# A linear attention beside a stack of local attentions: the first chunk's V copies go out early, and half of its Q is made ahead of the last output

## The chip, the cores and the metric

One core of one Trainium2 chip. The metric is the device time of one launch in microseconds, on the profiled core; the kernel is one program, with all data in SBUF between its start and its end except for the weights, the rotary tables and one copy of the input that is kept in DRAM.

## The reference

Input is x, 2048 tokens of 128 features. With xn the layer norm of x, the output is x + A(xn) + B(xn).

```python
def A(xn):                      # 8 heads of 16, one sequence of 2048
    q, k, v, gate = (xn @ W.T for W in (Wq, Wk, Wv, Wg))
    q, k = rope(q), rope(k)
    kv, ksum, vsum = einsum('bshd,bshe->bhde', k, v), k.sum(1), v.sum(1)
    o = (q @ kv * scale + vsum) / (q @ ksum * scale + 2048)
    return ((o + depthwise_conv5(v)) * gate) @ Wo.T

def B(x):                       # 6 layers, 16 heads of 64, windows of 32 tokens
    for i in range(6):
        q, k, v = split(shift_tokens(x) @ Wqkv[i], 3)
        q, k = l2norm(q) * qs, l2norm(k) * ks
        q, k = rope_xpos(q), rope_xpos(k)
        # each window of 32 queries sees its own 32 keys and the 32 before
        x = softmax(q @ k.T * 8 + mask) @ v @ Wo[i] + x
        x = ffn(shift_tokens(x)) + x       # layer norm, gated GELU, 341 wide
    return x
```

All is float32; some products are made of three matmuls on a high and a low part of each operand.

## The kernel before

**The start.** The input comes in as 16 tiles of 128 tokens. It is normalised on DVE and transposed into XA (128 features x 2048 tokens). Then A is computed: first Q, K and V of all tokens with the sums over K and V, then, in four groups (g = 0 to 3) of 512 tokens, the output. For a group TensorE makes the denominator and the numerator (`m_sums`), the convolution of V (`m_conv`, five matmuls, two records each in the trace), the gate (`m_gate`) and the output projection (`m_out`). ACT adds 2048 to the denominator (`m_den`). DVE inverts it and multiplies (`m_ratio`), adds the convolution and multiplies by the gate (`m_mix`, into `o1`), and adds the projection to the input (`m_add`, counted in `x1_done`). The sum x1 is written to DRAM (`scratch`) by one DMA and fetched again at the end.

**Chunks.** B runs over 6 layers x 8 chunks of 256 tokens, numbered m = 0 to 47. The work of a chunk is cut into steps: `a_...` is projection and preparation of Q, K and V, `b_...` scores, softmax and attention, `c_...` output projection and feed-forward part. A table, `SCHEDULE`, gives one order of steps, which every engine walks through with those of its own: in iteration `it` an a-step belongs to chunk `it`, a b-step to `it` - 1 and a c-step to `it` - 2, and `+1` behind a name means one chunk ahead. Each engine has its own instruction stream, and semaphores (named `..._done`, `..._in`) are all that ties them. `EARLY` names the steps of chunk 0 that aren't issued from the table because they are written out by hand between the group steps of A, as `a_v(0, 0)` and the like.

**Steps of a chunk that matter here.** `a_v`(m, c): V of half c on TensorE (6 matmuls of 512 columns, three for each half of the heads). `a_vs`: ACT copies it from PSUM to Vs, for which chunk m must wait until the V copies of chunk m - 1 have landed (`v2_in`). `windows`(m): SP issues 16 copies from Vs to V2, which lay V out by windows; V2 has two buffers, m % 2. `halo`(m): two more, the last window into the other buffer. `a_x`, `a_y`(m, p): a quarter of K (p = 0, 1) or Q (p = 2, 3) into PSUM bank 0 and 1; `a_mx`, `a_my`: DVE multiplies it by the rotary tables into UV; `a_sqx`, `a_sqy`: ACT squares it; `a_rot`: POOL adds up the rotated halves, into Kt or Qt (the first half of Qtb). `a_norm`, `a_rck`, `a_lnk`, `a_rh`, `a_rl`, `a_sp`: the K norms' inverse roots, spread over the partitions through TensorE; `a_kn`: DVE scales Kt by them. `keys`(m) and `queries`(m): SP issues 8 copies each, Kt to Kb and Qt to Qb. `b_s`(m, i): mask and scores on TensorE, which wait for `k_in` and `q_in`. `a_xs`, `a_xh`, `a_xl`: the shifted input of the next chunk and its high and low part, on ACT, ACT and POOL.

**SP's queue** is one stream, in program order; an instruction that waits holds all behind it. Before the chunks it ends in `keys(0)`, the write of x1 to `scratch` once `x1_done` is 4, and a wait until that has landed:

```python
keys(0)
e.wait_ge(s["x1_done"], G1)
e.dma_start(a["scratch"]..., xt).then_inc(s["scratch_out"], 16)
e.wait_ge(s["scratch_out"], 16)
for m in range(N):
    ...
    windows(m)
    if m:
        keys(m)
    queries(m)
    halo(m)
```

**Memory.** The start borrows space. `xt` (the input, later x1), `xn`, the convolution's weights `wc` and `lrow` lie in V2, whose first buffer is columns 0 to 4095 of `V2flat` and whose second is 4096 to 8191 (S is 2048). Input and normalised input fill the first buffer, so `windows(0)` can't be issued until the write of x1 has read it. `qT`, A's transposed Q, lies in the half of Qtb where chunk 0's Qt goes; `a_rot(0, 2)` waits for `x1_done`.

Of the kernel before, what the change touches and what calls it, by code (L numbers as in the profile page):

```python
# [18 lines left out]
S = 2048  # L19
D = 128  # L20
# [3 lines left out]
NCH = S // P  # L24
T1 = 512
G1 = S // T1
# [15 lines left out]
KLEPE = 5  # L42
# [23 lines left out]
    a_x1 a_y1 a_mx1 a_my1 a_sqy1 a_sqx1 a_rot1 a_norm0 a_sum0 a_rck0 a_lnk0 a_rh0 a_rl0 a_sp0 a_sp1 a_kn0 a_kn1""".split()  # L66
# [64 lines left out]
def program(nc, a):  # L131

    with ExitStack() as ctx:
# [60 lines left out]
        V2flat = V2[:, :, :, :].rearrange("p a w n -> p (a w n)")  # L194
        xt = V2flat[:, 0:S].rearrange("p (c n) -> p c n", c=NCH)
        xn = V2flat[:, S:2 * S].rearrange("p (c n) -> p c n", c=NCH)
        wc = V2flat[:, 2 * S:2 * S + KLEPE * D].rearrange("p (i n) -> p i n", i=KLEPE)
        lrow = V2flat[:, 2 * S + KLEPE * D:2 * S + 2 * KLEPE * D].rearrange("p (i n) -> p i n", i=KLEPE)
# [38 lines left out]
        def _(e):  # L237
# [98 lines left out]
            tables(1)  # L336
            keys(0)
            e.wait_ge(s["x1_done"], G1)
            e.dma_start(a["scratch"].rearrange("(c p) n -> p c n", p=P), xt).then_inc(s["scratch_out"], 16)
            e.wait_ge(s["scratch_out"], 16)  # L340
            for m in range(N):
                l, g = m // G, m % G
                if 0 < m < N - 1:
                    tables(m + 1)
                if g == 1 and l:
                    weights_b(l)
                if g == 2 and l:
                    weights_d(l)
                windows(m)
                if m:  # L350
                    keys(m)
                queries(m)
                halo(m)
                if g == 0 and l + 1 < DEPTH:
                    weights_a(l + 1)
                if g == 2 and l + 1 < DEPTH:
                    weights_c(l + 1)
# [10 lines left out]
        def _(e):  # L368
# [297 lines left out]
            a_v(0, 0)  # L666
            m_conv(0)
            m_sums(0)
# [21 lines left out]
            m_gate(3)  # L690
            m_out(3)
# [6 lines left out]
        def _(e):  # L698
# [221 lines left out]
            m_mix(3)  # L920
            m_add(3)
# [6 lines left out]
        def _(e):  # L928
# [193 lines left out]
            a_rh(0, 0)  # L1122
            run({"w_h": w_h, "c_wh": c_wh, "a_xs": a_xs, "a_xh": a_xh, "a_halo": a_halo, "a_vs": a_vs, "a_sqy": a_sqy, "a_sqx": a_sqx,
# [4 lines left out]
        def _(e):  # L1128
# [41 lines left out]
            def a_rot(m, p):  # L1170
# [3 lines left out]
                if m == 0 and p == 2:  # L1174
                    e.wait_ge(s["x1_done"], G1)
# [32 lines left out]
            a_rl(0, 0)  # L1208
            run({"b_nrm": b_nrm, "w_l": w_l, "c_wl": c_wl, "c_zl": c_zl, "a_xl": a_xl, "a_halo": a_halo, "a_rot": a_rot, "a_rl": a_rl, "b_sub": b_sub},
# [45 lines left out]
```

## Time and profile before

| what | value |
|---|---|
| median of 3 runs | 1840.32 us (1836.89 to 1849.28) |
| profiled execution, its own time | 1832.69 us |
| its span in the trace | 1831.1 us |
| mean granted clock of TensorE | 0.969 |
| instructions | 80253 |

The trace is of the profiled execution, and its times count from the start of the span. Engines are PE (TensorE matmuls), PEld (its weight loads), DVE, ACT, POOL; SPq is SP's queue issuing DMAs. Names in a row are tiles, output first: ps is PSUM, V stands for V2 and Vs's copies as well as for the input that lies in V2, E for the scores and, at the start, for A's intermediate results, Qtb at the start also for A's weights. Nearly all matmuls have the line of the helper `mm` (L370) and nearly all activations that of `act` (L930), so they are told apart by tile and shape. Behind a row of the timeline stands the idle time of the engine before it, and what ended it.

### The profile page before, as it was taken

Reading aid. Unit: us, or ns where it says so; the run is one execution under the profiler, and the core shown is the slowest. Engines: PE = TensorE matmul, PEld = TensorE weight load, DVE = VectorE, ACT = ScalarE, POOL = GpSimd, SP = SyncE. Lnnn points to the kernel's source line nnn. Section 1 sums busy time; section 2 is a strip of 40 time slices with the busy share of each in tenths; the row PEclk is TensorE's granted clock in tenths of the full one; section 3 lists DMA queues with packets and bytes.
Section 4 is the critical chain, followed back from the end, with each engine's and each line's share of the span. In section 5 each row is a group of like instructions: output and inputs, shape, how many; then the busy total and the mean of one; then the engine's idle time right before and its main releaser. Section 6 shows DMA issues by size and latency. Waiting matters only on the chain.

```text
span 1831.1 us, 80253 instructions
## 1 busy us (share of the span) xinstructions
PE 1654.4 (90%) x35762; PEld 1360.0 (74%) x35762; DVE 1217.9 (67%) x1910; ACT 1139.4 (62%) x2115; POOL 1000.9 (55%) x757
## 2 busy tenths in 40 slices
PE   5858999989989998899999999999999989999986
PEld 4447778777777877778777787777778777778775
DVE  7656677666657766666766775676677676677562
ACT  2225676657656766666766666576566676667653
POOL 2135466656545656655674664585566475566441
PEclk9979999999999999999999999999999999999996
DMA  3085665665655567556557655557655665665650
GB/s 124 12 199 126 165 145 132 149 170 127 152 136 134 127 157 194 114 130 158 133 125 194 154 129 138 139 130 188 162 129 128 152 141 123 154 152 127 140 120 24
DMA packets 98585, 253.25 MB, mean 138 GB/s; under 512 B 30016, under 2 KB 36288, under 8 KB 97472
## 3 DMA queue, kind: packets, MB, share of 16 engines
q1 hardware_dynamic: 98240, 248.12, 56.8%
q8 instruction: 281, 4.60, 1.1%
q14 instruction: 64, 0.52, 0.1%
HBM read 44.59 MB, written 2.10 MB: 25 GB/s over the span
## 4 chain that ended last, share of the span: by engine, by line
PE 54%; DVE 11%; issue 9%; ACT 9%; SPq 8%; DMA 2%; POOL 0%; ACTq 0%; DVEq 0%; POOLq 0%
PE ps L370 49%; DVE E L841 4%; SPq L317 4%; PE ps L539 4%; SPq L328 4%; DVE rs L851 3%; DVE UV L780 2%; ACT E L930 2%; ACT zs L930 2%; DMA Qtb<-Qtb 2%; ACT PT L930 1%; ACT sq L930 1%; ACT Vs L930 1%; PE ps L492 1%; ACT R L930 1%
## 5 line engine op out<-in xcount | busy, mean ns | idle before, releaser
L780 DVE SCALAR_TENSOR_TENSOR UV<-ps,veca,rope 128x512 f32<-128x512 f32 x768 | 526.7, 743 | 192.4 <-PE ps L370 191.5
L1183 POOL TENSOR_TENSOR Kt<-UV 128x512 f32<-128x512 f32 x192 | 240.8, 1275 | 446.5 <-DVE UV L780 445.3
L930 ACT ACTIVATE sq<-ps 128x512 f32<-128x512 f32 (+1 forms) x400 | 231.5, 579 | 321.7 <-PE ps L370 303.4
L1183 POOL TENSOR_TENSOR Qtb<-UV 128x512 f32<-128x512 f32 x192 | 242.6, 1286 | 123.5 <-DVE UV L780 123.5
L1193 POOL TENSOR_TENSOR E<-E,mx 128x1024 f32<-128x1024 f32 x96 | 182.7, 1903 | 148.4 <-DVE mx L847 148.4
L370 PE MATMUL ps<-xh,wh 128*128 128x256 f32 x768 | 242.2, 315 | 6.0 <-issue 4.4
L370 PE MATMUL ps<-xh,wl 128*128 128x256 f32 x768 | 221.9, 289 | 1.8 <-issue 1.8
L370 PE MATMUL ps<-xl,wh 128*128 128x256 f32 x768 | 221.5, 288 | 1.9 <-issue 1.9
L370 PEld LDWEIGHTS ps<-PT,V 64*64 64x64 f32 x12288 | 198.7, 135 | 31.6 <-issue 19.3
L370 PE MATMUL ps<-Kb,Qtb 64*32 64x64 f32 (+1 forms) x12288 | 189.3, 223 | 34.6 <-issue 34.5
L370 PE MATMUL ps<-PT,V 64*64 64x32 f32 x12288 | 215.9, 221 | 1.5 <-ACT PT L930 0.7
L370 PEld LDWEIGHTS ps<-Kb,Qtb 64*32 64x32 f32 x12288 | 154.0, 106 | 63.2 <-issue 63.0
L370 PE MATMUL ps<-OT,wo 128*128 128x128 f32 x1536 | 194.8, 281 | 4.4 <-issue 4.4
L1202 POOL TENSOR_TENSOR E<-E,ri 128x1024 f32<-128x1024 f32 x96 | 182.8, 1905 | 21.8 <-DVE ri L853 21.6
L370 PEld LDWEIGHTS ps<-OT,wo 128*128 128x128 f32 x1536 | 187.5, 199 | 5.1 <-issue 4.9
L370 PEld LDWEIGHTS ps<-xh,wh 128*128 128x128 f32 x768 | 150.9, 196 | 49.6 <-issue 26.5
L930 ACT ACTIVATE Vs<-ps 128x512 f32<-128x512 f32 x192 | 114.6, 598 | 92.1 <-PE ps L370 73.3
L851 DVE TENSOR_REDUCE rs<-E 128x16 f32<-128x1024 f32 x96 | 117.1, 1220 | 62.3 <-ACT E L930 62.3
L841 DVE TENSOR_TENSOR E<-ps,rq 128x1024 f32<-128x1024 f32 x96 | 114.9, 1197 | 64.6 <-PE ps L370 64.2
L539 PE MATMUL ps<-ident,E 128*128 128x128 f32 x768 | 123.0, 283 | 37.5 <-ACT PT L930 35.2
L370 PEld LDWEIGHTS ps<-xl,wh 128*128 128x128 f32 x768 | 151.7, 198 | 4.0 <-issue 4.0
L370 PEld LDWEIGHTS ps<-xh,wl 128*128 128x128 f32 x768 | 151.9, 198 | 2.8 <-issue 2.7
(129 smaller groups left out, 3324.1 us busy)
## 6 DMA issues: line engine op xcount, KB each, us to landing
V<-Vs SPq DMA_DIRECT2D x672, 128.0 KB
Kb<-Kt SPq DMA_DIRECT2D x384, 128.0 KB
Qtb<-Qtb SPq DMA_DIRECT2D x384, 128.0 KB, 2.4
rope<-in_c_rope SPq DMA_DIRECT2D x48, 512.0 KB
raw<-in_Wqkv SPq DMA_DIRECT2D x6, 1536.0 KB, 6.9
V<-Vs SPq DMA_DIRECT2D x96, 64.0 KB
V<-V SPq DMA_DIRECT2D x96, 64.0 KB, 2.0
wo<-in_Wo SPq DMA_DIRECT2D x6, 512.0 KB, 5.9
```

The lines of the kernel that those rows point to most:

```text
L317: e.dma_start(Kb[p0:p0 + W, j0:j0 + HQ, :], Kt[hq * W:(hq + 1) * W, half, :, :]).then_inc(s["k_in"], 16)
L328: e.dma_start(Qb[p0:p0 + W, j0:j0 + HQ, :], Qt[hq * W:(hq + 1) * W, half, :, :]).then_inc(s["q_in"], 16)
L370: return e.matmul(out, lhsT, rhs, start=start, stop=stop, **kw)
L492: ins = e.transpose(ps[:, NORM, T + c * P:T + (c + 1) * P], R[:, 1, c * P:(c + 1) * P], ident[:, :])
L539: ins = e.transpose(ps[:, PTB, h * P:(h + 1) * P], E[:, c, i % 2 * HQ + h, :, :], ident[:, :])
L780: e.scalar_tensor_tensor(UV[:, p % 2, slot, :].rearrange("p (i t) -> p i t", i=2), ps[:, half, :].rearrange("p (i t) -> p i t", i=2), veca ...
L841: e.tensor_tensor(E[:, c].rearrange("p j r k -> p r j k"), ps[:, 2:4, :].rearrange("p r (j k) -> p r j k", k=KEYS), by_row.unsqueeze(3).br ...
L851: e.tensor_reduce(rs[:, c], heads(E[:, c]), AX.X, ALU.add).then_inc(s["rs_done"], 1)
L930: return e.activation(out, in_, f, **kw)
L1183: e.tensor_tensor(dst, u, v, op).then_inc(s["rot_done"], 1)
L1193: e.tensor_tensor(ev, ev, mx[:, c].unsqueeze(2).broadcast_to([P, H, KEYS]), ALU.subtract).then_inc(s["sub_done"], 1)
L1202: e.tensor_tensor(ev, ev, ri[:, c].unsqueeze(2).broadcast_to([P, H, KEYS]), ALU.mult).then_inc(s["pn_done"], 1)
```

## The change

SP issues `windows(0)` right behind the tables, ahead of `keys(0)`, and no longer waits for the write of x1 ahead of the chunks; that wait stands ahead of `windows(1)`. To free the first buffer of V2, the input (`xt`) moves to the last quarter of V2, `wc` and `lrow` to behind the first 512 columns of the second buffer (which `halo(0)` writes), and `xn`, which is read early, to the front. The steps of the third quarter of chunk 0 (`a_x2` to `a_rot2`, half of its Q) join `EARLY`, and are written out ahead of `m_out(3)` on TensorE, `m_add(3)` on DVE and in the corresponding places on ACT and POOL. `a_rot(0, 2)` waits for the last numerator (`nm_done`), which is the last to read `qT`, instead of x1. On TensorE `m_sums(0)` goes ahead of `m_conv(0)`.

```diff
--- before.py
+++ after.py
@@ -63,7 +63,8 @@
     c_wl w_h2 c_fin c_down w_l2 b_oto1""".split()
 LAG = {"w": 0, "a": 0, "b": 1, "c": 2}
 EARLY = """a_xs0 a_xh0 a_xl0 a_halo0 a_v0 a_vs0 a_v1 a_vs1 a_x0 a_y0 a_mx0 a_my0 a_sqy0 a_sqx0 a_rot0
-    a_x1 a_y1 a_mx1 a_my1 a_sqy1 a_sqx1 a_rot1 a_norm0 a_sum0 a_rck0 a_lnk0 a_rh0 a_rl0 a_sp0 a_sp1 a_kn0 a_kn1""".split()
+    a_x1 a_y1 a_mx1 a_my1 a_sqy1 a_sqx1 a_rot1 a_norm0 a_sum0 a_rck0 a_lnk0 a_rh0 a_rl0 a_sp0 a_sp1 a_kn0 a_kn1
+    a_x2 a_y2 a_mx2 a_my2 a_sqy2 a_sqx2 a_rot2""".split()
 
 
 def part(token):
@@ -192,10 +193,11 @@
         hf = D // 2
 
         V2flat = V2[:, :, :, :].rearrange("p a w n -> p (a w n)")
-        xt = V2flat[:, 0:S].rearrange("p (c n) -> p c n", c=NCH)
-        xn = V2flat[:, S:2 * S].rearrange("p (c n) -> p c n", c=NCH)
-        wc = V2flat[:, 2 * S:2 * S + KLEPE * D].rearrange("p (i n) -> p i n", i=KLEPE)
-        lrow = V2flat[:, 2 * S + KLEPE * D:2 * S + 2 * KLEPE * D].rearrange("p (i n) -> p i n", i=KLEPE)
+        xt = V2flat[:, 3 * S:4 * S].rearrange("p (c n) -> p c n", c=NCH)
+        xn = V2flat[:, 0:S].rearrange("p (c n) -> p c n", c=NCH)
+        w0 = 2 * S + 512
+        wc = V2flat[:, w0:w0 + KLEPE * D].rearrange("p (i n) -> p i n", i=KLEPE)
+        lrow = V2flat[:, w0 + KLEPE * D:w0 + 2 * KLEPE * D].rearrange("p (i n) -> p i n", i=KLEPE)
         xr = raw[:, 0:S].rearrange("p (c n) -> p c n", c=NCH)
         Qt = Qtb[:, 0, :, :, :]
         Qb = Qtb[:, 1, :, :, :].rearrange("p h j t -> p (h j) t")
@@ -334,10 +336,10 @@
             weights_d(0)
             tables(0)
             tables(1)
+            windows(0)
             keys(0)
             e.wait_ge(s["x1_done"], G1)
             e.dma_start(a["scratch"].rearrange("(c p) n -> p c n", p=P), xt).then_inc(s["scratch_out"], 16)
-            e.wait_ge(s["scratch_out"], 16)
             for m in range(N):
                 l, g = m // G, m % G
                 if 0 < m < N - 1:
@@ -346,8 +348,10 @@
                     weights_b(l)
                 if g == 2 and l:
                     weights_d(l)
-                windows(m)
+                if m == 1:
+                    e.wait_ge(s["scratch_out"], 16)
                 if m:
+                    windows(m)
                     keys(m)
                 queries(m)
                 halo(m)
@@ -664,8 +668,8 @@
                 ins.then_inc(s["y1_done"], 1)
 
             a_v(0, 0)
+            m_sums(0)
             m_conv(0)
-            m_sums(0)
             a_v(0, 1)
             m_gate(0)
             m_sums(1)
@@ -688,6 +692,8 @@
             a_sp(0, 0)
             a_sp(0, 1)
             m_gate(3)
+            a_x(0, 2)
+            a_y(0, 2)
             m_out(3)
 
             run({"a_v": a_v, "a_x": a_x, "a_y": a_y, "a_norm": a_norm, "a_sp": a_sp, "b_rqt": b_rqt, "b_s": b_s, "b_pt": b_pt,
@@ -918,6 +924,8 @@
             a_kn(0, 0)
             a_kn(0, 1)
             m_mix(3)
+            a_mx(0, 2)
+            a_my(0, 2)
             m_add(3)
 
             run({"a_mx": a_mx, "a_my": a_my, "a_rck": a_rck, "b_rcq": b_rcq, "a_kn": a_kn, "b_rq": b_rq, "b_scale": b_scale,
@@ -1120,6 +1128,8 @@
             m_den(3)
             a_lnk(0, 0)
             a_rh(0, 0)
+            a_sqy(0, 2)
+            a_sqx(0, 2)
             run({"w_h": w_h, "c_wh": c_wh, "a_xs": a_xs, "a_xh": a_xh, "a_halo": a_halo, "a_vs": a_vs, "a_sqy": a_sqy, "a_sqx": a_sqx,
                  "a_lnk": a_lnk, "b_lnq": b_lnq, "a_rh": a_rh, "b_exp": b_exp, "b_pto": b_pto, "b_oto": b_oto, "c_xs": c_xs,
                  "c_zsq": c_zsq, "c_rs": c_rs, "c_zh": c_zh, "c_gelu": c_gelu}, lambda g: None)
@@ -1172,7 +1182,7 @@
                 if p == 0:
                     e.wait_ge(s["sel_done"], 4)
                 if m == 0 and p == 2:
-                    e.wait_ge(s["x1_done"], G1)
+                    e.wait_ge(s["nm_done"], G1)
                 if m and p % 2 == 0:
                     e.wait_ge(s["k_in" if p == 0 else "q_in"], m * 128)
                 q = 2 * (p % 2)
@@ -1206,6 +1216,7 @@
             a_rot(0, 0)
             a_rot(0, 1)
             a_rl(0, 0)
+            a_rot(0, 2)
             run({"b_nrm": b_nrm, "w_l": w_l, "c_wl": c_wl, "c_zl": c_zl, "a_xl": a_xl, "a_halo": a_halo, "a_rot": a_rot, "a_rl": a_rl, "b_sub": b_sub},
                 lambda g: None)
 
```

How it stands in each stream. SP, from the rotary tables of the start to the first chunk's Q copies (Vs to V: V copies; Kt to Kb: K copies; Qtb to Qtb: Q copies), before:

```order
L281 DMA rope<-in_c_rope 128x1024 x2
L317 DMA Kb<-Kt 32x1024 x8
L339 DMA scratch<-V 128x16x128
L292 DMA V<-Vs 32x1024 x4
L295 DMA V<-Vs 32x1024 x3
L297 DMA V<-Vs 32x512
L292 DMA V<-Vs 32x1024 x4
L295 DMA V<-Vs 32x1024 x3
L297 DMA V<-Vs 32x512
L328 DMA Qtb<-Qtb 32x1024 x8
L305 DMA V<-V 32x512 x2
```

and now:

```order
L283 DMA rope<-in_c_rope 128x1024 x2
L294 DMA V<-Vs 32x1024 x4
L297 DMA V<-Vs 32x1024 x3
L299 DMA V<-Vs 32x512
L294 DMA V<-Vs 32x1024 x4
L297 DMA V<-Vs 32x1024 x3
L299 DMA V<-Vs 32x512
L319 DMA Kb<-Kt 32x1024 x8
L342 DMA scratch<-V 128x16x128
L330 DMA Qtb<-Qtb 32x1024 x8
L307 DMA V<-V 32x512 x2
```

The V copies stand ahead of the K copies, and between the write and the Q copies nothing is left.

DVE, from the last denominator to the norms of chunk 0's Q (L780, now L786, are the multiplications by the rotary tables, four for each quarter; the row with V is the addition that makes x1), before:

```order
L809 TENSOR_SCALAR R<-ps 128x256
L772 TENSOR_TENSOR V<-ps,V 128x512
L824 TENSOR_TENSOR Kt<-ps,Kt 128x2x512 x2
L762 SCALAR_TENSOR_TENSOR E<-ps,Qtb,E 128x512
L767 TENSOR_TENSOR E<-ps,E 128x512
L772 TENSOR_TENSOR V<-ps,V 128x512
L780 SCALAR_TENSOR_TENSOR UV<-ps,veca,rope 128x512 x8
L809 TENSOR_SCALAR R<-ps 128x256
```

and now:

```order
L815 TENSOR_SCALAR R<-ps 128x256
L778 TENSOR_TENSOR V<-ps,V 128x512
L830 TENSOR_TENSOR Kt<-ps,Kt 128x2x512 x2
L768 SCALAR_TENSOR_TENSOR E<-ps,Qtb,E 128x512
L773 TENSOR_TENSOR E<-ps,E 128x512
L786 SCALAR_TENSOR_TENSOR UV<-ps,veca,rope 128x512 x4
L778 TENSOR_TENSOR V<-ps,V 128x512
L786 SCALAR_TENSOR_TENSOR UV<-ps,veca,rope 128x512 x4
L815 TENSOR_SCALAR R<-ps 128x256
```

Four of the eight multiplications stand ahead of the last addition.

TensorE, between the first and the second half of chunk 0's V (the rows with XA,V are the convolution, those with Qtb alone denominator and numerator), before:

```order
L370 MATMUL ps<-wl,xh 128x512
L370 MATMUL ps<-XA,V 128x512
L370 MATMUL ps<-XA,V 128x510
L370 MATMUL ps<-XA,V 128x511
L370 MATMUL ps<-XA,V 128x512 x2
L370 MATMUL ps<-Qtb 128x512 x2
L370 MATMUL ps<-wh,xh 128x512
```

and now:

```order
L374 MATMUL ps<-wl,xh 128x512
L374 MATMUL ps<-Qtb 128x512 x2
L374 MATMUL ps<-XA,V 128x512
L374 MATMUL ps<-XA,V 128x510
L374 MATMUL ps<-XA,V 128x511
L374 MATMUL ps<-XA,V 128x512 x2
L374 MATMUL ps<-wh,xh 128x512
```

The two matmuls of the sums went ahead of the five of the convolution.

## Rows read from the trace of the kernel before

**Rows 1.** The page, busy time by engine.

```profile
PE 1654.4 (90%) x35762; PEld 1360.0 (74%) x35762; DVE 1217.9 (67%) x1910; ACT 1139.4 (62%) x2115; POOL 1000.9 (55%) x757
```

**Rows 2.** The table by stretch: busy us and instructions, granted clock, DMA share, GB/s.

```profile
60.00:80.00 20.00, 18.94 (x75) 11.00 (x75) 19.36 (x19) 4.96 (x8) 2.50 (x2) 1.00 0.01 2
...
110.00:120.00 10.00, 3.27 (x9) 2.66 (x10) 0.00 (x0) 1.98 (x4) 0.00 (x0) 0.50 0.86 192
...
171.00:207.00 36.00, 33.78 (x805) 28.22 (x807) 26.46 (x41) 25.25 (x49) 22.07 (x17) 1.00 0.65 152
```

**Rows 3.** The chain in order of time: start, us, what.

```profile
97.98 5.40 DMA scratch<-V
...
114.04 2.02 DMA V<-Vs
```

**Rows 4.** Timeline of TensorE: start, us, engine, line, operation, tiles, shape.

```profile
60.51 1.02 PE L370 MATMUL ps<-XA,Qtb 128*128 128x512 f32 x2
...
63.45 1.13 PE L370 MATMUL ps<-Qtb 128*128 128x512 f32 x2 [1.06 <-DVE E L757]
...
89.74 0.36 PE L370 MATMUL ps<-Rh,sel 128*128 128x256 f32 x1 [0.40 <-issue]
...
94.34 1.86 PE L370 MATMUL ps<-Qtb,E 128*128 128x128 f32 x8 [2.55 <-DVE E L767]
...
106.32 0.80 PE L370 MATMUL ps<-wh,xh 128*128 128x512 f32 x1 [2.39 <-POOL xl L1161]
...
108.62 0.63 PE L370 MATMUL ps<-wl,xh 128*128 128x512 f32 x1
116.73 0.80 PE L370 MATMUL ps<-wh,xh 128*128 128x512 f32 x1 [7.48 <-ACT Vs L930]
...
122.08 0.41 PE L370 MATMUL ps<-mask,identb 32*32 32x512 bf16 x8
122.41 0.21 PE L370 MATMUL ps<-Kh,Qtb 64*32 64x32 f32 x1
```

**Rows 5.** Timeline of ACT.

```profile
60.02 1.29 ACT L930 ACTIVATE Vs<-ps 128x512 f32<-128x512 f32 x2 [0.87 <-PE ps L370]
```

**Rows 6.** Timeline of SP's queue; a row's us hold the issues and waits between.

```profile
13.02 32.41 SPq L281 DMA_DIRECT2D rope<-in_c_rope  x2
...
92.87 5.06 SPq L317 DMA_DIRECT2D Kb<-Kt  x8
...
114.68 5.04 SPq L328 DMA_DIRECT2D Qtb<-Qtb  x8
```

**Rows 7.** Timeline of DVE.

```profile
90.49 2.36 DVE L824 TENSOR_TENSOR Kt<-ps,Kt 128x1024 f32<-128x1024 f32 x2 [2.49 <-PE ps L370]
...
96.24 0.69 DVE L772 TENSOR_TENSOR V<-ps,V 128x512 f32<-128x512 f32 x1 [1.95 <-PE ps L370]
97.59 1.41 DVE L780 SCALAR_TENSOR_TENSOR UV<-ps,veca,rope 128x512 f32<-128x512 f32 x2 [0.66 <-PE ps L370]
...
100.77 2.90 DVE L780 SCALAR_TENSOR_TENSOR UV<-ps,veca,rope 128x512 f32<-128x512 f32 x4 [0.20 <-PE ps L370]
```

**Rows 8.** Timeline of POOL.

```profile
103.09 2.49 POOL L1183 TENSOR_TENSOR Qtb<-UV 128x512 f32<-128x512 f32 x2 [0.54 <-DVE UV L780]
105.54 0.72 POOL L1161 TENSOR_TENSOR xl<-xs,xh 128x256 fp32r<-128x256 f32 x1
```

**Rows 9.** The page, DMA issues: count, KB each, us to landing.

```profile
Qtb<-Qtb SPq DMA_DIRECT2D x384, 128.0 KB, 2.4
```

**Rows 10.** TensorE's waits, the chain, queues in 127 to 131, a stretch.

```profile
PE ps L370 <- issue: 52.8, 38, 3.3
...
127.35 3.28 issue
...
q8 instruction: 1, 0.02, 1.8%
...
131.00:136.00 5.00, 5.00 (x97) 3.90 (x83) 4.64 (x7) 1.80 (x5) 3.76 (x3) 0.66 1.04 211
```

## The prediction

> **What bounds the kernel now.** I read the page first. TensorE is busy 90% of the span [rows 1], so time goes where it stands idle or where it is the last to finish. The table by stretch then shows that the start is unlike the rest [rows 2]: in 110 to 120 us TensorE is busy for 3.27 of 10 us at a granted clock of 0.50 (all of it at the lower level, 1.2 GHz), DVE and POOL do nothing, and the DMA rings are busy for 0.86. From 171 us on TensorE is busy 33.78 of 36 us. The change touches only what is done once, in the first 125 us, so its worth is read there.
>
> The chain of waits goes through this place without a gap [rows 3]: SP issues the write of x1 to DRAM at 97.98, waits 5.40 us for it to land, then issues the first chunk's 16 V copies, and the last lands 2.02 us after 114.04, at 116.06. That releases ACT (V of chunk 1 out of PSUM into Vs, which the copies read), and that releases TensorE at 116.73, after 7.48 us of idleness [rows 4]. From there the chain is TensorE work, then chunk 1's K, Q and attention: each chunk follows from the one before, and no row shows a resource with a clock of its own. What comes off here should come off the end.
>
> **SP: V copies ahead of K copies, no wait for the write.** The V of chunk 0 is complete in Vs when ACT's pair from 60.02, 1.29 us long, ends at 61.31 [rows 5]. SP was through with its start-up loads at 45.43 (13.02 + 32.41, nearly all of it a wait) and then stood until the K copies at 92.87 [rows 6]. The 16 V copies take 16 x 0.63 = 10.1 us of issue (8 Q copies take 5.04 [rows 6]) and 2.0 to land: 61.4 to about 73.6, in a stretch where the rings' share is 0.01 [rows 2]. They cost nothing while they end before the K copies, at 92.87 less what the rest gains; more than 17 us of cover are left. What makes room for them, the input, the convolution's weights and the normalised input in other columns of V2, adds and moves no instruction. K copies are issued for 5.06 us as before, then the write, then SP goes straight to the Q copies. The wait for the write (5.40) stands now ahead of chunk 1's V copies, which come later anyway; the write lands before them. So the release at 116.06 goes and the 7.48 us go, if nothing else is late. Term C: 7.5, with 7.48 as the row gives it; below it only by what stands under "what is late next".
>
> **Half of Q ahead of the last output.** DVE finishes the key scaling (pair from 90.49) at 92.85, does the last mix, then idles 1.95 us for TensorE's last output, 0.66 for the first Q projection and 0.20 for the third [rows 7]: 2.8 us. Now its four Q multiplications stand between mix and output. Their projections need only PSUM banks 0 and 1, which the two key scalings free (about 1.2 and 2.36 us after their start), and TensorE has nothing else: it waits for the mix 2.55 us before 94.34 [rows 4]. Each projection is six matmuls of 256 columns. The six of 512 columns from 106.32 to 108.62 are 0.46 apart at the low clock [rows 4]; half the columns make 0.23, and six 1.4 us, an estimate. So the first is ready before DVE ends the mix, and TensorE is through with both soon after it and turns to the output. DVE runs through: four multiplications (2.9 as a row of four), the addition (0.69), four more. ACT's squares of the same PSUM banks fit beside them. The second pair of projections could be late by up to 0.7 us at the low clock. Term B: 2.8, bounds 2.0 (0.7 off for that, rounded) and 2.9. The output's addition ends about 0.8 us earlier than before in spite of the four, so the write is not held up: it follows the K copies, as before. POOL makes this half of Q before the other half, beside DVE, at the same length per pair; its new condition, the last numerator instead of x1, is met before. ACT makes xs of chunk 1 later, at about 95; what needs it, POOL's xl at 105.54, stands behind the last Q rotation anyway [rows 8].
>
> **Sums before convolution.** TensorE's first convolution stood ahead of the first sums, for which DVE waits. With the order turned DVE's first reciprocal begins earlier, but the first output still needs the gate, which TensorE issues at 60.51 behind the second V projection [rows 4], and that has not moved. What is gained is the idle 1.06 us before 63.45 and the turn it started: TensorE reaches its second numerator at about 61.8 instead of 63.45. It then has work without a gap of note (18.94 of the 20 us from 60 to 80 [rows 2]) up to R's broadcast at 89.74, where its own idle time is 0.40. So that broadcast and the key scaling come 1.6 us earlier. Term A: 1.6; 0 if DVE or ACT hold the chain at its old time, and no more than 1.6, as TensorE has no idle time to give.
>
> **What is late next.** With A + B = 4.4 the last Q rotation (POOL, pair from 103.09, end 105.58 [rows 8]) ends at 101.2 and xl at 101.9, so TensorE starts V of chunk 1 at 101.9 instead of 106.32 and goes on into its second half after 2.8 us (six times 0.46), in place of 116.73. Its work up to the scores of chunk 0 (122.08 masks, 122.41 first score) is then 11.9 us earlier, at 110.5. The scores also need Q: issued from 101.2, 5.04 us of issue, 2.4 to land [rows 6, 9], 108.6. So Q has 1.9 us to spare and is the next bound: whatever else gets faster here, the gain ends at 13.8. Chunk 1's V copies, behind Q copies and the next layer's weights, come about as much earlier as the scores do; their readers are a chunk later.
>
> **Sum:** 1.6 + 2.8 + 7.5 = 11.9 us. The profiled execution took 1832.69 (span 1831.1), so it would take 1820.8. That execution is 7.6 below the median of the three runs shown, 1840.32; taken off that median, the forecast is 1828.4. Own bounds: 0 + 2.0 + 7.5 = 9.5 and 13.8, so 1826.5 to 1830.8 on the same scale.
>
> **A rule against it.** TensorE stood 3.28 us at 127.35 "for nothing the profile shows"; the one packet of the instruction queue in 127 to 131 us is 0.02 MB [rows 10]. I read this as program code that came late. Moved copies could then uncover such a load elsewhere: in 61 to 73 us TensorE has few instructions (75 matmuls in 60 to 80 [rows 2]), so one at most, 3.3 off the gain.
> The Trainium skill, "Runtime: NRT & Kernel Launch", section Instruction fetch mechanics, says the opposite of such loads: the sequencer fetches the next block while it executes, and crossing a block is "mostly hidden". By that page the early copies cost nothing at all and the sum stays 11.9; by the row it could be 8.6. The same row shows the page's rule not holding at 127.35, if the packet is its cause.
>
> **Rivals.**
> 1. The write of x1 takes the place of the V copies. Now the Q copies follow it without a wait; it is issued at about 97 and lands 5.4 later, at 102.4, just as the Q copies start. If they are held by the whole 5.4, less the 1.9 they have to spare, 3.5 are lost: gain 8.4, 1831.9. For it: the rings share. Against: they overlap for 1.4 us only. 0.13.
> 2. More goes than the idle time. TensorE, no longer idle from 109 to 116.7, keeps the high clock up to the scores (gain 13.8, where Q caps it), the 3.28 us vanish, and the matmuls of 131 to 136, granted 0.66 [rows 10], gain 5 x 0.34 = 1.7: 18.8, 1821.5. Against: TensorE still waits from about 96 to 101.9 for most of the time, as before 106.32. 0.12.
> 3. The gain is used up inside chunk 1: some chain that hangs on the early part alone, not on the scores, sets its end; then A + B alone or less arrive, 0 to 4.4: 1836 to 1840. Against: the chain runs through the scores of chunk 0. 0.08. That the copies don't leave early would end here too; the order of SP says they do.
> 4. Slower: late code loads. The trace has 38 idle times of TensorE without a releaser, 52.8 us, the longest 3.3 [rows 10]. If SP's copies, now about 1.5 us ahead of TensorE's work in the early chunks, meet more of them, each costs the mean, 52.8 / 38 = 1.4. Nine use up the gain (11.9 / 1.4), 22 make it slower by 1%, and with 30 of the 48 chunks hit it is 30 x 1.4 - 11.9 = 30 slower, 1870. Against: each chunk's V copies wait for its own V, which sets the distance anew. 0.04.
> Forecast: 0.63.
>
> **Chances.** 1% (18.4 us) is about what a measurement of this kernel can tell from no change. Rival 2 is faster by more, and the three runs shown differ by 12.4, so a gain of 12 can be read as more than 18: faster 0.17. Forecast, rivals 1 and 3: same 0.80. Slower 0.03. The range: 1818 takes in rival 2 and some noise of the median, 1839 rivals 1 and 3 nearly whole.
>
> **What would show it.** After: no idle time of TensorE over 3 us between 103 and 120; V copies issued from 61.4; Q copies from 101; DVE without idle time from the key scaling to the last of eight multiplications; first score at 110.5; chunk spacing and busy shares unchanged after that. A wait for Q copies longer than 1 us before the scores speaks for rival 1, a first score before 109 for rival 2, unchanged end times with early scores for rival 3, a sum of releaserless idle time well above 52.8 for rival 4. Wrong altogether if the time differs by less than 4 or more than 20 us.

## The result, and the profile after

Over 14 runs of each on the same chips, the changed kernel took 1824.95 us in the median (1813.93 to 1842.36) and the kernel before 1838.81 (1827.73 to 1851.03). The ratio is 0.9912, 95% interval 0.9885 to 0.994: faster by 16 us, between 11 and 21. One of the 14, the longest, ran in a slower state and isn't in the ratio. A second measurement further down gave 0.9928 (0.99 to 0.9957), 13 us. The forecast was 11.9 off the time before, 1828.4 us; the time lies in its range, and the gain at the low end of the interval. My own bounds on the gain were 9.5 to 13.8; the medians differ by 13.9, and the two ratios give 13 and 16, so the gain is near the upper bound or above it. The profiled execution took 1818.27 us (span 1816.5), where that of before took 1832.69 (1831.1).

SP's queue after, from the V copies of chunk 0 on (start, us from first issue to last, line, tiles, count):

```profile
62.79 2.52 SPq L294 DMA_DIRECT2D V<-Vs  x4
...
73.60 0.60 SPq L299 DMA_DIRECT2D V<-Vs  x1
92.99 4.96 SPq L319 DMA_DIRECT2D Kb<-Kt  x8
98.00 0.59 SPq L342 DMA_DIRECT2D scratch<-V  x1
102.22 5.67 SPq L330 DMA_DIRECT2D Qtb<-Qtb  x8
```

The V copies end 19 us before the K copies start, as forecast. Against [rows 6], the Q copies start 12.5 us earlier, as POOL's last rotation ends (102.19, below), and no wait for the write stands before them. But their issue takes 5.67 us instead of 5.04.

TensorE after, the rows that answer to [rows 4]:

```profile
50.57 0.77 PE L374 MATMUL ps<-wh,xh 128*128 128x512 f32 x1 [3.60 <-POOL xl L1171]
...
89.86 0.35 PE L374 MATMUL ps<-Rh,sel 128*128 128x256 f32 x1 [0.40 <-issue]
...
94.46 1.16 PE L374 MATMUL ps<-Qtb,E 128*128 128x128 f32 x8 [0.46 <-DVE E L773]
96.40 0.38 PE L374 MATMUL ps<-xh,wh 128*128 128x256 f32 x1 [0.79 <-ACT sq L938]
...
102.93 0.50 PE L374 MATMUL ps<-wh,xh 128*128 128x512 f32 x1 [2.22 <-POOL xl L1171]
...
105.03 0.63 PE L374 MATMUL ps<-wh,xh 128*128 128x512 f32 x1
...
109.13 0.41 PE L374 MATMUL ps<-mask,identb 32*32 32x512 bf16 x8
109.70 0.21 PE L374 MATMUL ps<-Kh,Qtb 64*32 64x32 f32 x1 [0.16 <-DMA Qtb<-Qtb]
```

The 7.48 us of idleness before V's second half are gone: it starts at 105.03, right behind the first, where before it started at 116.73. The first score comes at 109.70 instead of 122.41. And its row names a new wait, 0.16 us for the Q copies: these are now the last to arrive, if only just. The two projections for Q's first half (ahead of 94.46) fill most of the time in which TensorE waited 2.55 us for the mix; 0.46 are left.

DVE and POOL after, for [rows 7, 8]:

```profile
90.61 2.35 DVE L830 TENSOR_TENSOR Kt<-ps,Kt 128x1024 f32<-128x1024 f32 x2 [2.50 <-PE ps L374]
...
94.32 2.72 DVE L786 SCALAR_TENSOR_TENSOR UV<-ps,veca,rope 128x512 f32<-128x512 f32 x4
96.95 0.68 DVE L778 TENSOR_TENSOR V<-ps,V 128x512 f32<-128x512 f32 x1
97.55 2.72 DVE L786 SCALAR_TENSOR_TENSOR UV<-ps,veca,rope 128x512 f32<-128x512 f32 x4
```

```profile
99.69 2.50 POOL L1193 TENSOR_TENSOR Qtb<-UV 128x512 f32<-128x512 f32 x2 [0.64 <-DVE UV L786]
102.15 0.72 POOL L1171 TENSOR_TENSOR xl<-xs,xh 128x256 fp32r<-128x256 f32 x1
```

Behind the scaling of the keys, none of DVE's rows has an idle time before it up to the eighth multiplication. But the scaling itself starts at 90.61, no earlier than the 90.49 of [rows 7], although the sums went ahead; why, the experiment with the convolution first shows.

The page, busy time by engine, and the table by stretch (as [rows 1, 2]):

```profile
PE 1650.2 (91%) x35762; PEld 1358.0 (75%) x35762; DVE 1220.4 (67%) x1910; ACT 1140.8 (63%) x2115; POOL 1001.9 (55%) x757
```

```profile
60.00:80.00 20.00, 20.00 (x80) 11.90 (x79) 16.39 (x18) 4.96 (x8) 2.50 (x2) 1.00 0.44 100
100.00:110.00 10.00, 7.62 (x83) 5.39 (x72) 2.23 (x5) 3.97 (x8) 2.87 (x3) 0.83 0.83 203
110.00:120.00 10.00, 7.64 (x316) 5.38 (x296) 8.66 (x12) 3.58 (x7) 7.59 (x6) 0.87 0.94 275
...
171.00:207.00 36.00, 34.06 (x801) 28.00 (x800) 24.60 (x38) 24.63 (x46) 20.93 (x17) 1.00 0.67 154
```

The V copies have filled an empty stretch (the share of time in which the DMA rings are busy is 0.44 instead of 0.01 in 60 to 80) beside a TensorE that is never idle there. The counts of instructions are as before and the later chunks nearly so; the granted clock of 110 to 120 us is 0.87 instead of 0.50. Finer stretches show when TensorE's clock fell and came back. Before:

```profile
104.00:105.00 1.00, 0.00 (x0) 0.00 (x0) 0.42 (x1) 0.00 (x0) 1.00 (x2) 0.92 0.51 115
...
121.00:122.00 1.00, 1.00 (x6) 0.93 (x5) 0.92 (x2) 0.14 (x1) 0.00 (x0) 0.54 0.50 129
```

and after:

```profile
103.00:104.00 1.00, 1.00 (x4) 0.84 (x5) 0.00 (x0) 0.00 (x0) 0.00 (x0) 0.84 0.67 147
...
107.00:108.00 1.00, 1.00 (x8) 0.87 (x7) 0.00 (x0) 0.58 (x2) 0.00 (x0) 0.95 0.83 184
```

Before, it fell to the lower level (1.2 GHz) at about 104.8 us, ahead of the first half of chunk 1's V, and stayed there through that half, the idle time and the second half, until about 121.9. After, it fell at about 103.7, in that first half, and was back at about 107.1.

The chain of after at the same place:

```profile
97.55 2.07 DVE UV L786 x3
...
99.69 2.51 POOL Qtb L1193 x2
102.22 0.51 SPq L330
...
107.30 2.35 DMA Qtb<-Qtb
...
109.70 1.03 PE ps L374 x36
```

It no longer goes through the write and the V copies [rows 3]; it goes through DVE, POOL and the Q copies.

### The profile page after: what moved, and what is told of

It reads as the page before. It is cut to its first block, busy times and chain, and to the rows that moved or that the text cites. A ratio compares the mean times of both kernels' runs of the same rounds, so it can differ in the third digit from the quotient of the medians.

```text
span 1816.5 us, 80252 instructions
## 1 busy us (share of the span) xinstructions
PE 1650.2 (91%) x35762; PEld 1358.0 (75%) x35762; DVE 1220.4 (67%) x1910; ACT 1140.8 (63%) x2115; POOL 1001.9 (55%) x757
## 4 chain that ended last, share of the span: by engine, by line
PE 50%; DVE 12%; SPq 11%; issue 9%; ACT 9%; DMA 3%; POOL 1%; ACTq 0%; DVEq 0%; POOLq 0%
PE ps L374 46%; SPq L330 5%; SPq L319 5%; DVE E L847 4%; PE ps L543 3%; DMA Qtb<-Qtb 3%; DVE UV L786 3%; DVE rs L857 2%; ACT E L938 2%; ACT zs L938 2%; ACT PT L938 1%; DVE Kt L830 1%; ACT sq L938 1%; PE ps L496 1%; ACT Vs L938 1%
## 5 line engine op out<-in xcount | busy, mean ns | idle before, releaser
L786 DVE SCALAR_TENSOR_TENSOR UV<-ps,veca,rope 128x512 f32<-128x512 f32 x768 | 526.8, 744 | 181.1 <-PE ps L374 180.3
```

Source lines behind the costliest of these rows:

```text
L786: e.scalar_tensor_tensor(UV[:, p % 2, slot, :].rearrange("p (i t) -> p i t", i=2), ps[:, half, :].rearrange("p (i t) -> p i t", i=2), veca ...
```

## The experiments

The profiles are read by three distances, since the start of V's projection of chunk 0 (S, the first matmul of wh and xh) itself drifts between 48.99 and 52.35 us: from S to the scaling of the keys (K, DVE), from K to POOL's xl, and from K to the first score. "Stop" is TensorE's idle time without a releaser in the second half of chunk 0's scores; "chunks 0 to 4" is the time between their rows of rq.

| kernel | S | S to K | K to xl | K to first score | stop | chunks 0 to 4 | ratio to before (95%) |
|---|---|---|---|---|---|---|---|
| before | 49.88 | 40.61 | 15.05 | 31.92 | 3.28 | 136.9 | 1 |
| before again | 50.20 | 40.28 | 15.09 | 31.62 | 2.81 | 138.8 | - |
| changed | 50.57 | 40.04 | 11.54 | 19.09 | 1.87 | 138.3 | 0.9912 (0.9885-0.994) |
| changed again | 49.20 | 40.15 | 11.53 | 19.13 | 2.32 | 140.0 | 0.9928 (0.99-0.9957) |
| V late | 52.35 | 39.68 | 11.53 | 30.81 | 1.74 | 141.0 | 0.9972 (0.9934-1.0009) |
| V early alone | 48.99 | 41.79 | 15.27 | 22.55 | 1.78 | 140.1 | 0.9925 (0.9894-0.9955) |
| convolution first | 49.64 | 41.55 | 11.54 | 19.16 | 1.98 | 142.2 | 0.9886 (0.9835-0.9938) |
| Q late | 51.24 | 40.23 | 13.59 | 21.79 | 4.47 | 142.6 | 0.9911 (0.9881-0.9941) |
| V behind K | 50.93 | 39.94 | 11.54 | 28.58 | 2.48 | 141.7 | 0.9977 (0.9948-1.0006) |
| wait kept | 50.75 | 39.95 | 11.54 | 20.09 | 2.18 | 143.0 | 0.9954 (0.9912-0.9995) |
| write behind Q | 50.12 | 39.91 | 11.54 | 18.85 | 2.05 | 143.2 | 0.9945 (0.9912-0.9979) |
| weights later | 50.85 | 39.05 | 11.53 | 19.14 | 0.46 | 143.8 | 0.9971 (0.994-1.0002) |
| before, weights later | 49.48 | 40.30 | 15.10 | 31.50 | none | 142.8 | 1.0061 (1.0029-1.0094) |

The distances behind K are good to some tenths (kernels that have the same steps there agree that well); S to K moves by more, as the experiment with the convolution shows. The ratios are good to 0.3 to 0.5%, 5 to 10 us.

### V late: everything but the V copies

```diff
-            windows(0)
             keys(0)
             e.wait_ge(s["x1_done"], G1)
             e.dma_start(a["scratch"]..., xt).then_inc(s["scratch_out"], 16)
+            e.wait_ge(s["scratch_out"], 16)
+            windows(0)
```

> The changed kernel with chunk 0's V copies put back behind the write of x1 and its wait; half of Q early and the sums first are kept. Additive theory (each term is worth its size alone: 1.6 + 2.8): first score of chunk 0 near 118, 4.4 us better than before. Chain theory (the V release hangs on the K copies and the write, which those two terms do not move in this trace: K copies from 92.99, write from 98.00): V copies from about 103.4, last landing 116.1, first score 122 +- 0.7, gain 0 to 0.7 us, ratio to before 1.000.

TensorE of this kernel:

```profile
104.34 0.50 PE L375 MATMUL ps<-wh,xh 128*128 128x512 f32 x1 [2.21 <-POOL xl L1172]
...
117.56 0.80 PE L375 MATMUL ps<-wh,xh 128*128 128x512 f32 x1 [10.65 <-ACT Vs L939]
```

V's first half comes as early against K as in the changed kernel, and then TensorE idles 10.65 us instead of 7.48 for the same late release. From K to the first score it takes 30.81 us: 1.0 less than before, where B by its own size would have 3.5 less; 0.4 of that 1.0 lies behind the wait, from V's second half to the masks (4.94 us instead of 5.35). From S it is 70.5 us, against 72.5, 71.9 and 71.8 in the three profiles that have all of the start as before: 1.3 to 2.0 earlier. That is over the 0 to 0.7 of the chain theory and far under the 4.4 of the additive one. The ratio can't be told from 1. The chain theory holds for Q: making half of it early is worth little as long as the V copies are late. It does not hold for the sums: the K copies wait for the scaling of the keys, so they move with it (issued 42.1 us behind S, before 42.7 to 43.0), and the write and the V copies behind them.

### V early alone

```diff
-    a_x2 a_y2 a_mx2 a_my2 a_sqy2 a_sqx2 a_rot2"""
...
-            m_sums(0)
             m_conv(0)
+            m_sums(0)
```

with the steps of chunk 0's third quarter taken out of the hand-written part on four engines; the memory layout stays the changed one.

> Only the V copies early, in the new memory layout; Q's first half and the convolution as before. Both theories: the 7.48 us before V's second half are gone, TensorE starts V of chunk 1 at 106.3 as before, first score near 114.6 (113.0 at the earliest, where Q copies from 105.6 end), gain 7.5 to 9 us, ratio about 0.9955.

```profile
106.82 0.79 PE L373 MATMUL ps<-wh,xh 128*128 128x512 f32 x1 [1.62 <-POOL xl L1164]
...
109.55 0.50 PE L373 MATMUL ps<-wh,xh 128*128 128x512 f32 x1
...
112.99 0.41 PE L373 MATMUL ps<-mask,identb 32*32 32x512 bf16 x8
```

This one edit takes 9.2 us from K to the first score (31.8, the mean of two profiles of before, to 22.55), of 7.5 to 9 expected. 7.3 is the idle time (7.48 and 7.16 in the two), and 1.9 is clock: from the start of V's second half to the masks it takes 3.44 us, before 5.35 (116.73 to 122.08 [rows 4]). It also has most of the gain in the total.

### Convolution first

```diff
-            m_sums(0)
             m_conv(0)
+            m_sums(0)
```

> The changed kernel with the first convolution ahead of the first sums again. If the sums first are worth my 1.6: key scaling at 92.1 instead of 90.61, first score 111.3 instead of 109.7. Rival: the swap gave nothing, as the same matmuls took 6.9 us instead of 6.1 (1.5 us of start-up drift aside): key scaling within 0.5 of 90.6, first score within 0.7 of 109.7. No difference in total that a run can tell.

From S to K, the five kernels with the convolution first take 41.55, 41.79, 40.61, 40.28 and 40.30, mean 40.9; the eight with the sums first 39.05 to 40.23, mean 39.9. But this mean of 1.0 mixes two things, and cutting the distance at the second half of chunk 0's V separates them. TensorE of the kernel before, convolution, sums and the start of that half:

```profile
52.57 4.99 PE L370 MATMUL ps<-XA,V 128*128 128x512 f32 x10
57.40 1.88 PE L370 MATMUL ps<-Qtb 128*128 128x512 f32 x4
58.71 0.80 PE L370 MATMUL ps<-wh,xh 128*128 128x512 f32 x1
```

and of this one:

```profile
52.34 5.93 PE L374 MATMUL ps<-XA,V 128*128 128x512 f32 x10
58.10 1.88 PE L374 MATMUL ps<-Qtb 128*128 128x512 f32 x4
59.42 0.80 PE L374 MATMUL ps<-wh,xh 128*128 128x512 f32 x1
```

The order is the same and nothing waits, but convolution and sums take 6.14 us in one and 7.08 in the other: TensorE's clock, at its lower level behind S, came back sooner in the kernel before (granted clock of 54 to 56 us: 1.00 there, 0.67 here). Over all profiles this stretch took 5.81 to 7.32 us with the convolution first and 5.92 to 7.08 with the sums first. From the second half of chunk 0's V to K, on the other hand, the five kernels with the convolution first took 31.77 or 31.78 us and the eight with the sums first 30.41 to 30.45. So the swap is worth 1.35 us, near the 1.6, and the return of the clock, up to 1.5 us sooner or later, is laid over it. In the changed kernel's first profile it can't be seen, since its S is 0.7 late and its stretch takes 6.91. The key scaling came at 91.19 rather than the 92.1 expected, with an S 0.9 earlier than the changed kernel's; in the distance, 1.5 longer, the first theory is right. Behind K nothing changes (19.16), and in the total a microsecond can't be seen: the 0.9886 is the lowest ratio of all, and its interval, from 6 runs, holds the changed kernel's.

### Q late

```diff
-    a_x2 a_y2 a_mx2 a_my2 a_sqy2 a_sqx2 a_rot2"""
+    """
```

and, again, the same steps taken out of the hand-written part.

> The changed kernel with all of Q behind the last output again. By the sum: DVE idles about 2.8 us again, last Q rotation at about 105, first score at 112.5 to 113.8 instead of 109.7 (the high clock before the scores gone too would make it 114), gain 9 us left, ratio 0.995. Rival (Q early is hidden under the V copies' gain): first score below 111.

The first score is at 113.26, within the 112.5 to 113.8 expected, and 21.79 behind K: Q early is worth 2.7 us there. With the convolution first it is worth 3.4 (V early alone 22.55, convolution first 19.16). The prediction's 2.8 was right for one and low for the other. Again the clock is a part of it. From K to xl it takes 13.59 us here and 15.05 before, with the same steps of Q. The table by stretch for 96 to 98 us, before and here:

```profile
96.00:98.00 2.00, 2.00 (x11) 2.00 (x11) 1.10 (x2) 0.00 (x0) 0.00 (x0) 0.50 0.92 205
```

```profile
96.00:98.00 2.00, 1.90 (x17) 1.69 (x15) 1.40 (x3) 0.07 (x1) 0.00 (x0) 1.00 0.97 215
```

Here Q's projections run at the higher level, before at the lower, and DVE idles 1.8 us in place of 3.0. So against Q late, with the clock high in both, Q early takes 2.05 us out of K to xl; the other 1.5 of the 3.5 against before is what this kernel has too, and the clock is the only difference there that the trace shows. Why it was low there in the four profiles with Q late and the convolution first, and high in this one, no run separates. In the total, 0.9911 against 0.9912, three microseconds are below what these runs tell.

### Before again

> The kernel before itself, a second profile. It tells what two executions of one program differ by. Expected: the start of V's projection of chunk 0 within 1.5 us of 49.88, first score 72.5 +- 0.7 us behind it as in the profile before; from there chunk times wander against the first profile by up to 5 us either way, without a trend. If the wandering of the gain after the first chunks (11.0 to 15.3 us) belonged to the change, the two profiles of before would keep within 1 us of each other.

S is 0.3 later, the first score 71.9 behind it instead of 72.5. But the span is 1840.9, 9.8 us longer than that of the first profile of the same program, and the distance grows: 1.6 us at chunk 4, 3.3 at chunk 8, 6.3 at chunk 11, 9.9 at chunk 47. That is twice the 5 us expected, and it has a trend, which I had not expected. So a span says little of a change of 12 us, and the wandering of the changed kernel's lead against before (13.0 us at chunk 0, 11.5 at chunk 4, 9.7 at chunk 18, 15.3 at chunk 23, 10.3 at chunk 47, 14.6 at the end) is of the size by which two executions of one program differ too. Only distances inside the first 125 us, and ratios of many runs, bear on the change.

### V behind K, and the write of x1

Three kernels move SP's steps. V behind K:

```diff
-            windows(0)
             keys(0)
+            windows(0)
```

> The changed kernel with chunk 0's V copies behind the K copies, still ahead of the write and without its wait: V copies from 98.0, last landed about 110; then write, then Q copies from 108.8, landed near 117. First score near 117, 26 us behind the key scaling instead of 19.1, gain about 5.5 us, ratio 0.997. If only the wait for the write mattered and not SP's idle time before 93 us, the first score would stay near 110.

Wait kept, ahead of the Q copies:

```diff
             e.dma_start(a["scratch"]..., xt).then_inc(s["scratch_out"], 16)
+            e.wait_ge(s["scratch_out"], 16)
             for m in range(N):
```

> The changed kernel with the wait for the write of x1 put back, now ahead of the Q copies. Write issued near 98.0, landed near 103.4: the Q copies start about 1.2 us later than 102.2, but no longer share the rings with it, so their issue takes 5.0 instead of 5.67: first score 0.3 to 0.9 us later in distance from the key scaling (19.1 us now). If the order and not the wait is what counts, the total keeps all but 1 us of the gain; if the wait is the half of it, 5 us are lost.

Write behind the Q copies and the halo of chunk 0:

```diff
-            e.wait_ge(s["x1_done"], G1)
-            e.dma_start(a["scratch"]..., xt).then_inc(s["scratch_out"], 16)
...
                 halo(m)
+                if m == 0:
+                    e.wait_ge(s["x1_done"], G1)
+                    e.dma_start(a["scratch"]..., xt).then_inc(s["scratch_out"], 16)
```

> The changed kernel with the write of x1 issued behind the Q copies and the halo. Rival 1 says the write holds the Q copies: their issue falls from 5.67 to about 5.0 us, the first score comes 0.2 to 0.7 us earlier (then TensorE's own work, masks at 109.1, is last). Chunk 1's V copies wait longer for the write, to about 118 instead of 110.9, and are through by the K copies at 131; no loss. Total within 1 us of the changed kernel.

V behind K, SP and TensorE:

```profile
109.16 0.58 SPq L342 DMA_DIRECT2D scratch<-V  x1
109.79 7.43 SPq L330 DMA_DIRECT2D Qtb<-Qtb  x8
```

```profile
111.22 0.79 PE L374 MATMUL ps<-wh,xh 128*128 128x512 f32 x1 [5.67 <-ACT Vs L938]
119.45 0.21 PE L374 MATMUL ps<-Kh,Qtb 64*32 64x32 f32 x1 [3.29 <-DMA Qtb<-Qtb]
```

The position counts and not the wait alone: without SP's idle time before 93 us the V copies hold TensorE 5.67 us, then the Q copies 3.29. It was slower than expected (28.58 from K, expected 26), because the write of x1, now right ahead of the Q copies, stretches their issue to 7.43 us. That is my first rival at work. In the changed kernel they are 4.2 us behind the write and it costs 0.7 of issue: 5.67 against 4.96 in the two kernels that keep the write away (and 4.95 where the Q copies come 6 to 8 us behind it, in Q late and V early alone):

```profile
104.00 4.96 SPq L330 DMA_DIRECT2D Qtb<-Qtb  x8
```

(wait kept) and

```profile
101.64 4.96 SPq L330 DMA_DIRECT2D Qtb<-Qtb  x8
```

(write behind Q). The first starts the copies 1.8 us later and loses 1.0, a little more than the 0.3 to 0.9 expected; the second wins 0.24 and is then held by TensorE's own work (its first score comes without a wait). Neither can be told from the changed kernel in total with these intervals; both ratios are higher in their centre. Taking the write out of the Q copies' way brings nothing that could be told, and no version here can be shown to beat the changed kernel.

### Changed again, and the weights later

The stop of TensorE in chunk 0's scores [rows 10] stands in all eleven profiles of the other kernels, 1.74 to 4.47 us long. To see whether it hangs on what is in the rings, the load of the next layer's QKV weights (1.5 MB, ahead of chunk 1's V copies) was put off by one chunk, in the changed kernel and in that of before:

```diff
-                if g == 0 and l + 1 < DEPTH:
+                if g == 1 and l + 1 < DEPTH:
                     weights_a(l + 1)
```

> The changed kernel itself again, unchanged. Key scaling 39.9 to 40.2 us behind the start of V's projection, first score 18.9 to 19.2 behind the key scaling; chunk 0 to chunk 4 (row of rq to row of rq) between 138 and 143 us, TensorE idle without a releaser at the stop in the second half of chunk 0's scores between 1.9 and 4.5 us. Ratio to before between 0.9885 and 0.994, as in the first measurement.

> The changed kernel with the load of the next layer's QKV weights (1.5 MB) one chunk later in each layer, so that it no longer goes out just ahead of chunk 1's V copies. Late-code theory (the stop of TensorE in the second half of chunk 0's scores, 1.9 to 4.5 us in eight profiles, is a block of program code that arrives late behind full rings): the stop falls below 1.5 us, chunk 0 to 1 takes 34 us or less, total 2 to 4 us better than the changed kernel's second run beside it. Rival (the stop has nothing to do with what is in the rings): the stop stays at 1.9 to 4.5, total unchanged.

> The kernel before with the same later weight load. Late-code theory: the stop of 3.28 us at 127.35 falls below 1.5 us and the kernel is 2 to 4 us faster than before, ratio 0.998 to 0.999; rival: stop unchanged, ratio 1.000. Either way it stays 9 us or more behind the changed kernel, since the V release at 116 us is as late as it was.

TensorE with the weights later, in the changed kernel: at the old place (chunk 0's scores) first, and one chunk on:

```profile
114.43 1.08 PE L374 MATMUL ps<-Kb,Qtb 64*32 64x64 f32 x86 [0.46 <-issue]
...
148.58 0.58 PE L374 MATMUL ps<-xh,wh 128*128 128x256 f32 x1 [4.10 <-issue]
157.06 0.60 PE L374 MATMUL ps<-Kb,Qtb 64*32 64x64 f32 x36 [0.92 <-issue]
```

and SP's load there:

```profile
141.11 0.45 SPq L256 DMA_DIRECT2D raw<-in_Wqkv  x1
```

In the kernel before:

```profile
160.54 0.58 PE L370 MATMUL ps<-xh,wh 128*128 128x256 f32 x1 [3.51 <-issue]
```

The changed kernel's second run came out as expected in all its numbers (table). Where the weights left, the stop fell to 0.46 or went altogether (chunk 0 to 1 took 32.4 us instead of 34.3 in the changed kernel; 32.5 in that of before, instead of 33.6 and 32.9 in its two profiles). Where they went, a stop that was there already grew: at the place of the 4.10 and 3.51 us the eleven other profiles have 1.84 to 2.78. Chunk 1 to 2 took 42.0 instead of 36.4 and 41.0 instead of 35.9. The load costs more in its new place, and the totals are worse: by 0.4% against the second run of the changed kernel beside it (0.9971 and 0.9928, intervals that just overlap), and by 0.6% against before. Half of the expectation failed: the stop does hang on the traffic, but no time was won by moving it.

## Why the prediction was right, and where it was off

**The bound and the chain: right.** The release of V's second half was the piece on the path; it went, and the first score came 12.7 us earlier in the first profiles (13.4 from S), of 11.9 forecast. The V copies are hidden in SP's idle time, and V behind K shows what they cost without it.

**Term C, 7.5: too small by the clock.** TensorE took 10.41 us from V's first half to its second (106.32 to 116.73), and 2.10 after: 8.3 gone. I had the six matmuls at the low clock's 0.46 us; the first three ran at the high one, before it fell at 103.7. So did what follows: 4.10 from the second half to the masks, where it had been 5.35. Together that is 9.6 us where I had 7.5. The step that was mis-sized is "goes on into its second half after 2.8 us" and its work up to the scores "11.9 us earlier": it carried over the durations of the clock's lower level. Before, the clock had fallen ahead of V's first half and did not come back until 121.9; without the idle time it was back at 107.1. I had put this into rival 2, as a high clock kept up to the scores. That came true in part, for the clock still was low for 3.4 us; its other two parts didn't: the stop stayed at 1.87 and the low clock later in chunk 0 too (0.50 in 118 to 123 us).

**Term B, 2.8: measured 3.5** from K to xl (15.05 to 11.54). I had left out one wait of DVE, 0.16 us for ACT. The waits by themselves are worth less than I summed, 2.05 us by Q late; the other 1.5 came with the clock, since before TensorE had made the last output and the first projections of Q at the lower level (0.50 in 95 to 98 us), and in the changed kernel it didn't.

**Term A, 1.6: measured 1.35**, from the second half of chunk 0's V to K, and not to be seen in one profile from S. I took the stretch ahead of it as fixed; the sums and convolution took 53.27 to 60.18, 6.9 us, where they had taken 6.1 (52.57 to 58.71). That is the return of the clock and not the swap, as the convolution first shows. 0.6 us is left of A in the first profiles.

**What is late next: right.** Q copies last, with the spare used up: TensorE had its masks out 1.0 us sooner than forecast (109.13 for 110.2), the last rotation ended 1.0 later (102.19 for 101.2), and the write took 0.7 of the copies' issue. That is more than the 1.9 I gave, and yet the wait is only 0.16 us, since by luck I had counted 7.4 us from the first issue to landing where undisturbed copies take 6.8 (wait kept, 104.00 to 110.79). 3.5 + 8.3 + 1.25 is 13.1, less 0.24 for the longer way from masks to score: 12.8, which is the difference from K (31.92 to 19.09). With the 0.6 of A it is 13.4 from S, against 11.9. My cap of 13.8 on the gain held.

**How much was luck.** Counted apart from the clock, the waits that went are worth 1.35 + 2.05 + 7.5 = 10.9 us, a little less than the 11.9. The clock, which the sum held to be as before, added 1.5 in B and 2.1 behind it, and took 0.8 in the convolution and sums ahead of the second half of chunk 0's V. The mechanism was the one I named; that the number is near is in part that these two misses have opposite signs.

**The sum as a sum: right only in this order.** I wrote the terms as if each had its own worth, and in rival 3 gave "A + B alone" 4.4 us. V late shows 1.3 to 2.0 from S: 0.6 to 0.9 of it ahead of K, where A works, 0.7 to 1.1 behind K, and 0.4 of the latter by the clock. B moves TensorE forward to a wait that ends at the same time; A moves what that wait hangs on.

**Rivals.** 1: true in mechanism, small here (0.7 of issue), 2.5 us where the write stands right ahead. 2: the clock part. 3 and 4: no. There are 38 idle times without a releaser after as before; the sum is 50.8 us, not above 52.8. (The second profiles have 41 with 55.8 us, and 44 with 56.5 for the kernel before, so it tells little to some microseconds.) One thing stays open: chunks 0 to 4 took 138.3 to 143.2 us, mean 141.4, in the eight kernels with V early and the weights in place, and 136.9, 138.8 and 141.0, mean 138.9, in the three with V late. Some two of the thirteen microseconds may be given back there; three against eight values that overlap don't settle it, and it was not tried further.

**The rule weighed against the row.** The stop hangs on what is in the rings: it shrank where the 1.5 MB load left and grew where it went. That it is program code that comes late fits this, but was not shown. That crossing into a new block of code is mostly hidden is what the Trainium skill has under "Runtime: NRT & Kernel Launch", section Instruction fetch mechanics; if the stop is such a crossing, the rule did not hold here beside such a load, with 1.74 to 4.47 us, and no run shows whether it is. The early V copies uncovered no stop: TensorE was busy for all of 60 to 80 us.

**The chances.** Within 1% with 0.80: the ratio's centre is 0.9912, and its interval reaches both sides of 0.99. The medians differ by 13.9 us, 0.75%. A gain of 13 to 16 us is near the 18.4 of 1%, so a result above 1%, which I gave 0.17, was not far off.

## What to carry to other kernels

Look for a queue that stands idle before the place where its transfers are waited for, and ask what binds them there; here it was a buffer that a late reader still held, and laying that data elsewhere was all that it took. Terms on one chain add only if the last arrival moves with them: name for each term what releases the instruction behind it, and expect nothing of the others while that stays. And where an idle time of TensorE of several microseconds goes, take the durations around it from rows at the high clock as well as the low one, since the clock can come back sooner with it. To size a small edit, cut the distance at every mark between which the instructions are the same, so that a stretch in which the clock moved doesn't hide one in which the edit did.

## What the runs showed of the hardware

- Two executions of one program differed by 9.8 us of 1831, spread over many chunks, and the same first step (S) came at 48.99 to 52.35 us in thirteen profiles.
- A write of 1 MB to DRAM lengthened the issue of eight 128 KB copies behind it from 4.96 to 5.67 us when issued 4.2 us ahead of them, and to 7.43 when 0.6 ahead.
- TensorE stopped for 1.7 to 4.5 us without a releaser at one place of its program in eleven profiles. With a load of 1.5 MB moved away from it the stop was 0.46 us or none, and where the load went a stop of 1.84 to 2.78 us grew to 4.10 and 3.51.
- V's second half to the masks took 3.4 to 4.4 us without idleness before it and 4.5 to 5.4 behind 5.7 to 10.7 us of idleness, the same instructions at another granted clock.
- The same fourteen records of matmuls behind the first half of chunk 0's V took 5.81 to 7.32 us without a wait, by when the granted clock came back from 0.50 to 1.00.
